# Constants of the two-expert tiles: made by GpSimd in its fourth step, 66 inner rows for 97, and ScalarE's weight copies moved to the end of the second attention pass

## What is computed

```python
x = x + elu(attention0(layernorm(x), adj))     # graph attention, layer 0
x = x + mixture0(layernorm(x))                 # 8 experts, hidden 256, top 2, softmax weights, exact gelu
x = x + relu(attention1(layernorm(x), adj))    # graph attention, layer 1
# second mixture: 32 experts, hidden 32, top 1
idx = argmax(xf @ router_w.T + router_b)
h   = relu(xf @ W1[idx] + b1[idx])
x   = x + relu(h @ W2[idx] + b2[idx])
```

## Time and profile before

| | |
|---|---|
| median of 3 runs | 1121.83 us |
| the profiled execution's own time | 1121.34 us |
| its span, first to last instruction | 1119.6 us |
| mean granted clock of TensorE | 0.881 of full speed |
| stage 1, attention 0, with the routing tables | about 0 to 325 us |
| stage 2, first mixture | about 340 to 650 us |
| stage 3, attention 1 | about 650 to 900 us |
| stage 4, second mixture and stores | about 917 to 1119.6 us |

### The profile page before, as it was taken

The page is one execution under the profiler, slowest core; times in us unless marked ns, Lnnn a source line. Parts: engine busy times, 40 slices in busy tenths (PEclk is TensorE's granted clock), DMA queues, the critical chain, the costliest instruction groups (busy, mean ns, idle before and its releaser), DMA issues. The chain is left out here.

```text
span 1119.6 us, 26953 instructions
## 1 busy us (share of the span) xinstructions
PE 888.0 (79%) x6709; PEld 797.9 (71%) x6709; DVE 794.6 (71%) x3521; ACT 699.1 (62%) x2364; POOL 761.7 (68%) x975
## 2 busy tenths in 40 slices
PE   4788988988618999999999759999999518878810
PEld 3567777877618999999999747888888406666610
DVE  7779899888846999999999716888888823422310
ACT  2799899888504665566556459999998306653300
POOL 3327777677762887877888811787878846777776
PEclk9899899889758999999999979999999659985555
DMA  8323432221157888887878321223221145433311
GB/s 197 54 83 123 141 123 85 70 58 47 35 114 198 210 208 209 210 208 206 213 204 207 94 67 29 74 84 85 79 78 50 41 104 146 117 99 104 90 33 38
DMA packets 144935, 129.21 MB, mean 115 GB/s; under 512 B 26552, under 2 KB 116541, under 8 KB 144785
## 3 DMA queue, kind: packets, MB, share of 16 engines
q1 hardware_dynamic: 124144, 91.94, 33.2%
q0 software_dynamic: 17760, 34.20, 9.0%
q10 hardware_dynamic: 2880, 1.35, 0.6%
HBM read 82.74 MB, written 47.48 MB: 116 GB/s over the span
## 5 line engine op out<-in xcount | busy, mean ns | idle before, releaser
L507 POOL DMA_INDIRECT xs<-staged,dst x256 | 258.1, 1008 | 77.2 <-issue 68.6
L1168 ACT ACTIVATE hT<-bank,wt 128x128 f32<-128x128 f32 x620 | 177.3, 368 | 130.9 <-PE bank L1383 114.6
L538 POOL DMA_INDIRECT x2d<-ob,xi x155 | 161.0, 1038 | 43.0 <-issue 28.7
L560 POOL DMA_INDIRECT out<-oq,xq x144 | 142.9, 992 | 58.4 <-issue 42.7
L1369 PE MATMUL bank<-xnT,wt 128*128 128x128 f32 x1240 | 166.0, 277 | 0.0
L1383 PE MATMUL bank<-w2s,hT 128*128 x1240 | 164.0, 275 | 0.7 <-DVE ob L1041 0.5
L1369 PEld LDWEIGHTS bank<-xnT,wt 128*128 128x128 f32 x1240 | 152.8, 194 | 0.1
L1383 PEld LDWEIGHTS bank<-w2s,hT 128*128 128x128 f32 x1240 | 150.9, 192 | 1.0 <-issue 1.0
L1117 ACT ACTIVATE p<-bank,nm 128x128 f32<-128x128 f32 x256 | 103.2, 403 | 27.0 <-DVE nm L743 27.0
L1118 ACT ACTIVATE p<-bank,nm 128x128 f32<-128x128 f32 x256 | 104.8, 410 | 0.0
L1131 ACT ACTIVATE rl<-bank,rinv 128x128 f32<-128x128 f32 x256 | 97.1, 453 | 3.1 <-DVE staged L735 3.1
(11 more groups left out here) (250 smaller groups left out, 2203.3 us busy)
## 6 DMA issues: line engine op xcount, KB each, us to landing
wt<-wpd SPq DMA_DIRECT2D x155, 258.0 KB
xi<-xs SPq DMA_DIRECT2D x155, 66.0 KB
xq<-xs SPq DMA_DIRECT2D x144, 66.0 KB
xb<-x2d SPq DMA_DIRECT2D x32, 258.0 KB, 3.1
xb<-in_x SPq DMA_DIRECT2D x32, 256.0 KB, 3.9
wpd<-w1c SPq DMA_DIRECT2D x56, 129.0 KB
xs<-staged,dst POOLq DMA_INDIRECT x256, 2.5
x2d<-ob,xi POOLq DMA_INDIRECT x155
```

What stands on the lines that cost most here:

```text
L507: pool.indirect_dma_start(out=xs[l], out_offset=bass.IndirectOffsetOnAxis(ap=dst[b % ND][:, c:c + 1], axis=0), in_=stag[s][:, q, 0:ROW], i ...
L538: pool.indirect_dma_start(out=x2d, out_offset=bass.IndirectOffsetOnAxis(ap=xi[t % NXI][:, ID:ID + 1].bitcast(U32), axis=0), in_=ob[:, t % ...
L560: pool.indirect_dma_start(out=orow, out_offset=bass.IndirectOffsetOnAxis(ap=xq[j % NXQ][:, q, ID:ID + 1].bitcast(U32), axis=0), in_=oq[j % ...
L1168: last = act.activation(hT[t % 2][:, j, :], HID[t % 2][:, j, :], ACT.Gelu, bias=wt[t % NW][:, c:c + 1])
```

## The change

DVE no longer fills `hrT`, `w2d` and `side` and no longer makes `placef` and `place`; its two memsets of `hqT` stay. The two bias rows stand directly behind the 64 hidden rows, so `KD` is 66 and `w2d` is filled by DMAs alone. POOL makes `side`, `hrT`, `placei`, `placef` and `place` in step 4 of layer 0. ACT copies only into `vt` in steps 6 and 7, and makes `w1d` from `vt` behind `graph_layer(1)`. SP waits for `vt_zero` once. The new semaphores `sides` and `w1d` guard the new readers.

```diff
-KD = 2 * H1 + 33
+KD = 2 * H1 + 2
...
-            sp.wait_ge(sem("vt_zero"), 2)
+            sp.wait_ge(sem("vt_zero"), 1)
...
-            for k in range(2):
-                const("meet_in", w2d[2 * H1 + 32 * k:2 * H1 + 32 * k + 1, :, :], b2_1.rearrange("(o r k) d -> o r k d", o=1, k=2)[:, :, k, :])
+            const("meet_in", w2d[2 * H1:KD, :, :], b2_1.rearrange("(r k) d -> k r d", k=2))
...
-            pool.iota(placei[:, :], pattern=[[1, P]], base=0, channel_multiplier=0)
...
+                    if l == 0 and i == 4:
+                        pool.memset(side[:, :], 1.0)
+                        for s in range(2):
+                            pool.memset(hrT[s][0:KD, :], 1.0)
+                        pool.iota(placei[:, :], pattern=[[1, P]], base=0, channel_multiplier=0).then_inc(sem("sides"), 1)
+                        for k, (cut, sign, value) in enumerate(((H1, -1, -1.0), (2 * H1, -1, 1.0))):
+                            pool.wait_ge(sem("sides"), 1 + k)
+                            pool.affine_select(out=side[:, :], in_=side[:, :], compare_op=ALU.is_gt, fill=value, base=cut,
+                                               pattern=[[0, 1]], channel_multiplier=sign).then_inc(sem("sides"), 1)
+                        pool.wait_ge(sem("sides"), 3)
+                        pool.affine_select(out=side[:, :], in_=side[:, :], compare_op=ALU.not_equal, fill=-1.0, base=-(2 * H1 + 1),
+                                           pattern=[[0, 1]], channel_multiplier=1)
+                        pool.tensor_scalar(placef[:, :], placei[:, :], 0.5, None, ALU.add).then_inc(sem("sides"), 1)
+                        pool.wait_ge(sem("sides"), 4)
+                        pool.tensor_tensor(place[:, :], placef[:, :], side[:, 0:1].broadcast_to([P, P]), ALU.mult).then_inc(sem("sides"), 1)
...
-                    link(dve.memset(hrT[s][2 * H1:2 * H1 + 32, :], 0.0))
-                    dve.memset(hrT[s][2 * H1:2 * H1 + 1, :], 1.0)
-                    dve.memset(hrT[s][2 * H1 + 32:KD, :], 1.0)
-                for k in range(2):
-                    last = dve.memset(w2d[2 * H1 + 32 * k:2 * H1 + 32 * k + (32, 1)[k], :, :], 0.0)
-                last.then_inc(sem("vt_zero"), 1)
-                for k in range(4):
-                    dve.memset(side[32 * k:32 * k + 32, :], (1.0, -1.0)[k % 2])
...
-                dve.tensor_copy(placef[:, :], placei[:, :])
...
-                dve.tensor_scalar(place[:, :], placef[:, :], 0.5, side[:, 0:1], ALU.add, ALU.mult)
...
+                    if j == SINGLE:
+                        dve.wait_ge(sem("sides"), 5)
...
-                    act.activation(w1d[:, (k - 4) * 8:(k - 3) * 8, :], TP[:, :].rearrange("p (r h) -> p r h", r=8), ACT.Copy)
...
             graph_layer(1)
+            for k in range(2):
+                last = act.activation(w1d[:, :, k * H1:(k + 1) * H1], vt[:, :, 0:H1].rearrange("p (r k) h -> p r k h", k=2)[:, :, k, :], ACT.Copy)
+            last.then_inc(sem("w1d"), 1)
             fills(1)
...
+                else:
+                    act.wait_ge(sem("sides"), 1)
...
+                        if j == SINGLE and q == 0:
+                            pe.wait_ge(sem("w1d"), 1)
```

More of the change, by code:

```diff
@@ L1173, in _ @@
             act.wait_ge(sem("v2_in"), 16 * 3)
-            act.wait_ge(sem("meet_in"), 16 * 4)
+            act.wait_ge(sem("meet_in"), 16 * 3)
             def copies(j):
@@ L1389, in _ @@
             pe.wait_ge(sem("v2_in"), 16 * 3)
-            pe.wait_ge(sem("meet_in"), 16 * 4)
+            pe.wait_ge(sem("meet_in"), 16 * 3)
             for i in range(QUADS + 2):
```

## The result

The changed kernel takes 1113.26 us (median of 13 runs, 1111.46 to 1119.04); the kernel before took 1123.45 us in the 13 runs beside them. The ratio is 0.9922, with a 95% interval of 0.9907 to 0.9937: about 8.8 us less, 7.1 to 10.4 (the two medians lie 10.2 us apart, a measure of how far the single number can be trusted). The forecast was 1112.1 us, 9.7 us less. The profiled execution has a span of 1110.8 us for 1119.6.

The account below looks back on a forecast made before the run. DVE's memsets at 18 to 30 us of layer 0 were taken to hold up all other engines; 5.70 + 2.88 + 1.00 + 0.10 = 9.7 us off gave 1112.1 us, range 1109.0 to 1115.8 us.

Parts of the forecast that it names:

- The wait for `w1g`: Start of layer 0: PE's first spare product starts at 26.25 us instead of 31.95, 5.70 us gained.
- The clock: First spare product to turn of `pm`: with no idle time ahead PE keeps the upper level, 2.88 us more.
- ACT's copies: Steps 6 and 7: two copies into `w1d` removed, 0.50 us each counted whole, 1.00 us gained; bounds 0 and 1.2.
- `placei`: Its iota leaves the place ahead of POOL's `vt` memset, so DVE's cast of `adj_i` ends earlier; 0.1 us gained.
- POOL's block: Step 4: POOL's new work, 2.4 to 4.2 us, fits in 6.02 us of idle time; price 0.
- SP's queue: Loads of `vt`, `b1d` and `w2d` go out at about 19 us, first read in step 6; cost nothing.
- ACT behind layer 1: Two copies of about 0.6 us each fit in 9.2 us before ACT's fill DMAs; price 0.
- A: Step 4: POOL's new block holds DVE's residual, 3.0 us lost, 6.7 us gained, 1115.1 us; chance 0.13.
- B: Clock gives nothing back, or something holds PE after 26 us; 5.8 to 6.8 us gained, 1115.5 us; chance 0.08.
- C: More than forecast, for instance fewer lower-clock stretches in later steps: 11.5 us or more gained, about 1109 us; chance 0.05.
- D: From about 96 us, more lower-clock dips eat the gain: slower by over 0.5% 0.03, mostly eaten within 0.5% 0.04.
- E: Gain lost for want of input, since all loads have less time; no change to speak of; chance 0.02.

Follow-up runs that it names:

- the filler run: The kernel before, with six 128x512 products that nobody reads put on PE ahead of its wait for `w1g`; ratio 0.9989 (0.9972 to 1.0006).

## Why the prediction was right, point by point

**What bounded the start: right.** Step 0's memsets on DVE were all that the other engines waited for, and with them gone the layer starts earlier as a whole: statistics at 19.63 us for the forecast 19.95, exponentials at 21.61 for 21.9 to 22.6. The shift is still there at the end of the kernel.

**The wait for `w1g`, 5.70 us: right.** Forecast was a spare product at 26.25 us. Over the executions of the unaltered changed kernel it starts at 25.31, 25.97 and 26.57 us, and at the end of PE's own work each time. The slack of 2.2 us or more was 25.31 - 23.05 = 2.26 us, and more where PE was later; three memsets put into it cost nothing.

**The clock, 2.88 us: right,** both in cause (the filler run) and size (2.83 us for 5.71). This is nearly a third of the gain, and no instruction was removed for it. What the forecast did not have is that the clock's first rise, at 19 to 21 us by the products' lengths, moves by itself and shifts the start by up to 1.3 us. With it taken out, as above, the shift at step 5 is 8.76, 8.82 and 8.68 us in the three executions (the third has 8.94 us and 9.50 us between its `wcat` products), for 5.70 + 2.88 + 0.10 = 8.68 us forecast.

**ACT's copies, 1.00 us: mis-sized.** 0.36 us. The step that failed is "I count both whole": ACT had no gap in step 7 either, but there DVE, with its first routing, waits for nobody and ends the step, and time freed on ACT does not reach it.

**`placei`, 0.1 us: right,** though one pair of executions could not show it: PE's first `wcat` product starts at 15.43 to 15.58 us in three executions with the iota ahead of the memset, and at 15.26 to 15.48 us in seven without, on average 0.16 us earlier.

**POOL's block, price 0: right,** 3.4 us within the forecast 2.4 to 4.2. Wrong was what stands behind it, that beyond 6.02 us each us would cost one: a power that was 3.2 us late cost nothing.

**SP's queue, ACT behind layer 1, 66 rows: right,** as far as the trace shows; none of them releases anything late.

**The sum.** With 0.36 for 1.00 it would be 9.0 us; measured are 8.8 (7.1 to 10.4). The timing alone could not have told 9.0 from the forecast 9.7; that the terms are right is known from the marks and the runs above. The rest lies within what the way through layer 0 and the last stage do by themselves.

**The rivals.** A fell: the residual's ops took 0.69 us under POOL's block and under a block of 5.66 us of memsets. B fell with the 2.83 us. C and D are one mechanism seen from two sides; it exists, one dip at 60 us made ACT's wait 1.66 us and the step 0.84 us longer in the changed kernel's profiled execution (9.85 for 9.01 us), but over layer 0 the way varies by some 4 us and not 16. E fell: no DMA became a releaser of `xs_` or of the statistics in layer 0.

## What to carry to other kernels

Look at the first microseconds of a software pipeline for constants that one engine makes while all others wait; what is saved there is saved once but kept to the end, and it is worth what the second-latest engine allows, not what was removed. Where TensorE idles ahead of a burst, count the wait and then look whether the burst ran at the lower clock (behind 5.54 us of idle time it did here, behind 0.52 us it did not). Time freed on a busy engine is worth its full length only in steps that this engine ends: check each step for its own last engine before multiplying by the number of steps.

## What the runs showed of the hardware that was not expected

A long memset on GpSimd held a VectorE cast from int32 to fp32 until it was over. Under the memset of 4.38 us the cast ended 0.08 to 0.09 us behind it wherever it had started (4.24 us from 9.47 us in the changed kernel, 3.63 us from 9.95 us in the one without the ScalarE part); with the memset cut short it took 0.22 us. GpSimd's memsets did not hold VectorE's ops with two SBUF inputs: `qq` and `staged` took 0.68 and 0.69 us in the middle of 5.66 us of them. The Trainium skill, "GPSIMD Engine Reference", Specifications, names contention with VectorE's instructions in a two-port mode and with those with two SBUF inputs. Of the second kind none was held here by a memset; whether the cast is of the first kind no run here shows.

The other way round GpSimd's own small `placef` took 0.54 us in nine executions of the changed kernel and its variants, but 0.98 us in the run with twelve memsets on POOL, the only one in which it started, at 49.97 us, under DVE's `qq` (49.87 us, 0.69 us). `placef` reads SBUF, a memset does not; that this is the difference was not tested.

And the time at which TensorE's products first run at the upper level's speed is not fixed by the program: with the same instructions from 15.4 us on it came at about 19 us in one execution and about 21 us in another, and the start of the pipeline moved with it.
